# A fused linear-attention and FFN layer: the row sums of squares by one transpose instead of matmuls with ones

## The reference, cut to what matters

```python
xn = _layernorm(x)
x = x + attn(xn) + ffn(xn)
# attn, at its end; o, shift, final_gate: [B, T, 512]
o = gla_chunk_scan(q * SCALE, kn, v, rt_log)
o = o + shift * residual_weight
xg = o * silu(final_gate)
rms = rsqrt(mean(xg * xg, axis=-1) + 1e-5)
o = xg * rms * norm_weight
return o @ down_w.T
# ffn: three gated or plain layers of 1024, and w3 back to 256
```

## Time and profile before

| | us |
|---|---|
| median of 3 runs | 1967.26 |
| lowest, highest | 1966.08, 1968.8 |
| profiled execution, its own time | 1966.91 |
| its span, first to last instruction | 1965.0 |
| TensorE busy (matmuls) | 1947.1 |
| VectorE busy | 1581.9 |
| ScalarE busy | 1266.0 |
| GpSimd busy | 68.4 |

### The profile page before, as it was taken

How to read it: one execution, slowest core, us unless ns; L and a number is a source line. 1 busy time by engine, 2 the same in 40 slices (tenths; PEclk the granted TensorE clock), 3 DMA queues, 4 the chain that set the end, 5 groups by cost and what they waited for, 6 DMA issues and landing times.

```text
span 1965.0 us, 46591 instructions
## 1 busy us (share of the span) xinstructions
PE 1947.1 (99%) x17348; PEld 1932.8 (98%) x17348; DVE 1581.9 (81%) x4274; ACT 1266.0 (64%) x2527; POOL 68.4 (3%) x104
## 2 busy tenths in 40 slices
PE   7999999999999999999999999999999999999998
PEld 7999999999999999999999999999999999999998
DVE  7787878878788887887878788787888878878777
ACT  5665656666566666666656566666666666666564
POOL 0000000000000000000000000000000000000000
PEclk9999999999999999999999999999999999999999
DMA  8000000000000000000000000000000000000000
GB/s 305 7 12 12 12 7 6 12 12 12 12 1 12 12 12 12 12 1 12 12 12 12 7 6 12 12 12 12 1 12 12 12 12 12 2 12 12 12 7 8
DMA packets 23360, 34.22 MB, mean 17 GB/s; under 512 B 2945, under 2 KB 19713, under 8 KB 23186
## 3 DMA queue, kind: packets, MB, share of 16 engines
q1 hardware_dynamic: 23186, 31.46, 4.8%
HBM read 23.07 MB, written 8.39 MB: 16 GB/s over the span
## 4 chain that ended last, share of the span: by engine, by line
PE 95%; issue 2%; DVE 1%; ACT 1%; SPq 1%; DMA 0%; POOLq 0%; POOL 0%; DVEq 0%; ACTq 0%
PE fb L364 64%; PE ab L364 22%; PE ab L568 2%; PE ab L601 1%; PE ab L509 1%; PE ab L498 1%; PE ab L434 1%; PE fb L649 1%; PE ab L561 0%; SPq L272 0%; PE ab L580 0%; DVE hid0l L944 0%; PE ab L560 0%; DMA small<-stage_w 0%; ACT raw L805 0%
## 5 line engine op out<-in xcount | busy, mean ns | idle before, releaser
L364 PE MATMUL fb<-hid1h,wwhole 128*128 128x256 f32 x2048 | 475.0, 280 | 1.1 <-DVE hid1l L861 1.1
L364 PE MATMUL fb<-hid1l,wwhole 128*128 128x256 f32 x2048 | 468.5, 277 | 0.0
L364 PE MATMUL fb<-hid0l,wwhole 128*128 128x256 f32 x2048 | 465.9, 276 | 0.0
L364 PE MATMUL fb<-hid0h,wwhole 128*128 128x256 f32 x2048 | 465.8, 276 | 0.0
L364 PEld LDWEIGHTS fb<-hid1h,wwhole 128*128 128x128 f32 x2048 | 384.7, 188 | 3.8 <-ACT hid1h L720 0.8
L364 PEld LDWEIGHTS fb<-hid1l,wwhole 128*128 128x128 f32 x2048 | 384.9, 188 | 0.0
L364 PEld LDWEIGHTS fb<-hid0l,wwhole 128*128 128x128 f32 x2048 | 384.6, 188 | 0.0
L364 PEld LDWEIGHTS fb<-hid0h,wwhole 128*128 128x128 f32 x2048 | 384.5, 188 | 0.0
L805 ACT ACTIVATE raw<-fb,sh_s 128x256 f32<-128x256 f32 x512 | 212.7, 467 | 127.0 <-PE fb L364 124.8
L364 PE MATMUL fb<-xntl,wwhole 128*128 128x256 f32 x1024 | 237.5, 277 | 0.0
L364 PE MATMUL fb<-xnth,wwhole 128*128 128x256 f32 x1024 | 237.5, 277 | 0.0
(11 more groups left out here) (217 smaller groups left out, 4514.0 us busy)
## 6 DMA issues: line engine op xcount, KB each, us to landing
xin<-x SPq DMA_DIRECT2D x32, 256.0 KB, 2.7
out<-xin SPq DMA_DIRECT2D x32, 256.0 KB, 2.6
stage_more<-stage_w SPq DMA_DIRECT2D x6, 512.0 KB, 7.3
sgate<-stage_w SPq DMA_DIRECT2D x4, 512.0 KB, 5.5
shift<-stage_w SPq DMA_DIRECT2D x4, 512.0 KB, 5.6
v<-stage_w SPq DMA_DIRECT2D x4, 512.0 KB, 5.8
raw<-stage_w SPq DMA_DIRECT2D x3, 512.0 KB, 6.1
mixed<-stage_w SPq DMA_DIRECT2D x3, 512.0 KB, 8.5
```

Source lines behind the costliest of these rows:

```text
L364: mm = pe.matmul(o, a, b, start=start and i == 0, stop=stop and i == len(pairs) - 1)
```

## The change

The squares are written as two groups of 64 partitions. `sq` becomes [128, 8, 128]: partitions 0 to 63 hold chunk 0 and partitions 64 to 127 chunk 1, and the eight blocks are the four channel blocks of either half of the source's partitions. This takes four Squares of 64 partitions and 4 x 128 elements, for chunk c and source half r. VectorE then reduces eight blocks to `sqsum`, now [128, 128]: partition k of group c holds a partial sum of chunk c for each token. One fp32 transpose puts the tokens on the partitions and the 2 x 64 partial sums along them, in `fb[1]`, and a second VectorE reduction, out of PSUM, gives `total`, [128, 2]. `msq` is made from `total`, behind a wait for it. The bank `fb[1]` is read by the reduction and no longer by `msq`; TensorE still waits for `msq_d` before it writes there.

```diff
-        sq = work[:, 0:DB * N].rearrange("p (d t) -> p d t", d=DB)
+        sq = work[:, 0:NC * DB * CH].rearrange("p (d t) -> p d t", d=NC * DB)
         xn = work[:, DB * N:DB * N + NC * H].rearrange("p (c h) -> p c h", c=NC)
-        sqsum = work[:, DB * N + NC * H:]
+        sqsum = work[:, DB * N + NC * H:DB * N + NC * H + CH]
...
+        total = sb("total", [P, NC])
...
-        sq_d, xg_hi, ln_hi = sig("sq_d", 1), sig("xg_hi", 1), sig("ln_hi", 1, 1)
+        sq_d, xg_hi, ln_hi = sig("sq_d", NC * NC), sig("xg_hi", 1), sig("ln_hi", 1, 1)
...
-        sqsum_d = sig("sqsum_d", 1)
+        sqsum_d, total_d = sig("sqsum_d", 1), sig("total_d", 1)
...
                 pe.wait_ge(sqsum_d.sem, sqsum_d.at(me))
                 pe.wait_ge(gelu2_d.sem, gelu2_d.at(me, 4))
-                for c in range(NC):
-                    mm = pe.matmul(fb[1][:, c:c + 1], sqsum[:, c * CH:(c + 1) * CH], ones[:, 0:1], start=True, stop=True)
-                mm.then_inc(rs_mm.sem, 1)
+                pe.transpose(fb[1][:, 0:P], sqsum, ident_s[:]).then_inc(rs_mm.sem, 1)
...
-                act.activation(sq[:], sgate[:], ACT.Square).then_inc(sq_d.sem, 1)
+                for c in range(NC):
+                    for r in range(NC):
+                        act.activation(sq[rows(c), r * DB:(r + 1) * DB, :], sgate[rows(r), :, c * CH:(c + 1) * CH],
+                                       ACT.Square).then_inc(sq_d.sem, 1)
...
                 dve.wait_ge(rs_mm.sem, rs_mm.at(me))
-                dve.tensor_scalar(msq[:], fb[1][:, 0:NC], 1.0 / DI, EPS, ALU.mult, ALU.add).then_inc(msq_d.sem, 1)
+                dve.tensor_reduce(total[:], fb[1][:, 0:P].rearrange("p (c k) -> p c k", c=NC), mybir.AxisListType.X,
+                                  ALU.add).then_inc(total_d.sem, 1)
+                dve.wait_ge(total_d.sem, total_d.at(me))
+                dve.tensor_scalar(msq[:], total[:], 1.0 / DI, EPS, ALU.mult, ALU.add).then_inc(msq_d.sem, 1)
```

## The result

The changed kernel takes 1971.42 us (median of 14 runs, 1967.67 to 1974.03), the kernel before in the same session 1967.8 (14 runs, 1966.08 to 1968.8). The ratio is 1.0018, with a 95% interval of 1.001 to 1.0025. So the change made the kernel slower by a little under 4 us, where 9.5 us of gain were forecast. The profiled execution took 1969.75 us with a span of 1968.0, 3.0 more than before.

What follows compares the result with a forecast made beforehand. TensorE, busy 1947.1 of 1965.0 us, was taken as the bound: 31 halves by 0.325 gain 10.1 us, less 0.6 for the tail, 9.5 off 1966.91, so 1957.4; with 0.35 to the median, 1957.8 us, range 1955.8 to 1962.5.

Steps and rivals of the forecast that it cites:

- Slack 0.37: First halves: the reduction ends at 109.34, a load could start at 109.41, TensorE needs it at 109.78; no wait.
- slack 0.6: Second halves: squares start at 164.63, passes at 169.46, 4.83 us later instead of 4.59, so TensorE does not wait.
- all of the 0.325: TensorE, end of each half: four ones passes of 0.45 us become one transpose of 0.125, gaining 0.325 us.
- the sums come 1.47 later: ScalarE: four Squares in sequence take 2.52 us against one of 1.05, so the squares are ready 1.47 us later.
- I take 1.62: VectorE's long reduction to 128 sums of eight, priced per sum: 1.62 us instead of 2.02, bounds 1.62 to 2.15.
- Rival 1: VectorE's long reduction keeps its length or grows, 2.02 to 2.15 us, delaying TensorE in first halves; 1958.7 to 1960.9; chance 0.32.
- The switch to the next half's 16-column loads I price at nothing: TensorE, from the transpose to the next half's first loads: no added cost, as behind the ones passes.
- The tail: Last half, no TensorE work behind it: VectorE's path sets the end, msq at 1960.15 instead of 1959.60, 0.55 us later.
- the PSUM reduction: VectorE's new reduction over 128 PSUM elements ahead of msq: 0.30 us, plus 0.06 for the wait between the two.
- what was said to catch up: VectorE's convolution taps, delayed to 114.3, end at 115.98, before the z low's input at 116.18; lateness gone within one stage.
- the second: ScalarE's four squares take 0.9 us each, so TensorE waits for the sums; 1975.3 us at 1.0 us later; chance 0.05.
- The third: TensorE gains little: the transpose costs as much as four passes, or its next wait returns the gain; 1967.9 us; chance 0.10.

Runs made afterwards that it cites:

- late-sums run: The kernel before, ones passes kept, with its one Square cut into four of 64 partitions; 1975.74 us against 1968.2, ratio 1.0033.
- half-squares: The changed kernel with squares of only half the source's partitions, two Squares and a reduction over four blocks; 1961.54 us against 1968.43, ratio 0.9955.
- two-transpose: The kernel before, one Square and 256 sums, with two transposes and a PSUM reduction replacing the ones passes; 1971.7 us, ratio 1.0006; again 1964.53, ratio 0.9972.
- squares-ahead run: The changed kernel with squares and reduction moved ahead of the next input's high and low parts; 1968.44 us against 1968.2, ratio 1.0002.
- side-by-side: The changed kernel with a token's eight squares adjacent, so the reduction reads neighbours and ScalarE writes at a stride; 2034.37 us, ratio 1.0332.
- rounded-ones: The kernel before with sums and ones in the short rounded format, one pass per chunk instead of two, no transpose; 1965.62 us, ratio 0.9972.

## Why the prediction was wrong

**The step that failed: "Slack 0.37. In the second half ... slack 0.6. No wait, so all of the 0.325 stays."** The slack was measured to the load that uses the sums. Ahead of a turn of the loop, the deadline is earlier: the next half starts 0.93 us behind the release of the last wait in the loop's body, and what stands between, one transpose or four passes, runs within that time. Before, the sums were ready 2.19 us ahead of the next half, and the sums come 1.47 later, as I had worked out. With 0.325 less of TensorE's work in between, 2.19 - 1.47 - 0.325 = 0.40 us would have been left. The turn wants 0.93, so 0.53 us are lost; measured are 0.57 (60.03 against 59.71 - 0.25). The late-sums run shows it with nothing else changed, the half-squares and two-transpose runs show it gone with early sums, the squares-ahead run moves the sums and the next half moves along, and the loop's exit, which takes no turn, doesn't lose it. Why a turn takes this long no record shows. The Trainium skill (Runtime: NRT & Kernel Launch, Instruction fetch mechanics) says that a taken branch whose target is not among the instructions at hand waits for a fetch; a fixed time behind the last wait agrees with that, and no run here varied the length of the loop.

**"I take 1.62" for the reduction was mis-sized: 2.01.** The reading as a price per sum was wrong; the half-squares and side-by-side runs show a price per strided read. Rival 1 had the size right and the place too small: its 0.03 us in first halves came out as 0.08, and it saw nothing at the turns. With 1.62 the sums would have been 0.39 earlier, and 0.14 of the 0.53 would still be lost at each turn.

**"The switch to the next half's 16-column loads I price at nothing" was mis-sized by 0.08 us** in each half. Of 0.325 us some 0.24 stay: first halves went from 59.49 to 59.25, and the half-squares run's second halves from 59.71 to 59.47.

**The tail was mis-sized**: from the last square's start the prediction put msq 0.55 later. It starts at 1961.76, which is 0.96 later from there (0.4 of it the reduction) and 1.02 from the first load of the last half. The store of the output behind it landed 3.8 us after its issue instead of 3.0, which no run explains.

**What held.** Four squares of 0.629 us (0.635 taken), the sums' lateness in front of the reduction, the transpose's load of 0.14 and its own place in the queue, the PSUM reduction of 0.288 (0.30 taken). msq is never waited for, and what was said to catch up does so. VectorE ahead of and at the stage of the earlier trace rows:

```profile
112.30 0.29 DVE L1184 TENSOR_REDUCE total<-fb 128x2 f32<-128x128 f32 x1
112.62 0.17 DVE L1187 TENSOR_SCALAR msq<-total 128x2 f32<-128x2 f32 x1
113.66 0.88 DVE L1191 SCALAR_TENSOR_TENSOR xin<-ab,rms,xin 128x256 f32<-128x256 f32 x2 [0.87 <-POOL rms L350]
114.46 1.66 DVE L974 SCALAR_TENSOR_TENSOR shift<-xbuf,convw_s,shift 128x256 f32<-128x256 f32 x4
116.15 0.42 DVE L863 TENSOR_TENSOR zs<-ab,zs 16x256 fp32r<-16x256 f32 x1
```

The taps run together. Counted from the half's first load, z's low part starts at 6.44 us instead of 6.30 (116.15 - 109.71, 116.51 - 110.21), and TensorE doesn't wait for it.

**The sum, as it came out**, in the profiled spans: first halves at -0.24 each make -3.9; four stretches +3.3; a stall of 2.1 us near the end that only the kernel before has, -2.1; second halves +0.31 at 14 turns, with the last exit that does not turn, +4.1; tail +1.8; start -0.3. That is +2.9, against 3.0 between the spans. Held against the forecast instead (-0.325 in every half, +0.55 in the tail), the 14 second halves with a turn cost 0.636 x 14 = 8.9 us more, the exit 0.1, the first halves 0.08 x 16 = 1.3, the stretches 3.3 and the tail 1.25, less 2.1 and 0.3: 12.5, where the profiled execution is 12.4 above its forecast of 1957.4.

That stall was in nobody's sum. In the straight code of the last sequence, 34 us into its first half, ScalarE stands idle with no cause shown, and TensorE then waits for what it delivers, so that this half lasts 61.67 us instead of 59.49. Before:

```profile
1872.67 0.84 ACT L805 ACTIVATE raw<-fb,sh_s 128x256 f32<-128x256 f32 x2 [1.82 <-issue]
```

It is no accident of one execution: all five traces of kernels with the one Square have it (1.71 to 1.82 us of ScalarE), and none of the eight traces of kernels with two or four Squares. Why is open. So some 2 us of the comparison with before speak for the changed kernel, and for the half-squares and squares-ahead runs, for a reason that has nothing to do with the transpose; without them the loss would be larger.

**Of the rivals,** the second had the right form, TensorE losing to late sums, with the wrong cause (slow squares) and the wrong place. The third came nearest in size, with 1967.9, which is luck: the turns, the stretches, the tail and the stall happen to add up to little. Its break behind the transpose is what the rows show at a turn, but it doesn't belong to the transpose: the late-sums run has it behind the four passes. Where the two-transpose and the rounded-ones kernels beat both (0.9972 in the session where they were measured together), the first of them was level with before in another session, so a gain of some 3 us is likely for these and not settled. What makes TensorE fall from one distance to the other is open: the late load is necessary in all that was seen of h1, not sufficient, and it doesn't explain the stretches elsewhere.

## What to carry to other kernels

A wait that stands right ahead of a loop's turn has its deadline at the release, not at its instruction: measure the time from release to the first instruction of the next iteration, and keep late results (here those that come less than some 0.93 us ahead of the next iteration) away from that place. Before making a producer later to make a consumer shorter, look for the variant that shortens the consumer alone, as the single-pass ones did here. And count what a cheaper instruction does to its neighbour's start: a quarter of the gain went there.

## What the runs showed of the chip that was not expected

- The turn on TensorE: 0.92 to 0.94 us (medians; single turns 0.83 to 1.00) from the end of the reduction that releases the last wait to the next iteration's first load, in five kernels.
- Passes of 256 columns, of the same form and at a granted clock of 1.00, follow each other at 113.3 or at 117.8 ns for some 18 us of the h1 layer and 6 at the half's end, which makes 0.8 to 0.9 us in a half. Four and eight more such halves make 3.3 of 4.2 us and 7.4 of 7.5 us between two traces of one program; executions without a trace differ by up to 11 us, most likely for the same reason.
- An idle time of 1.7 to 1.8 us on ScalarE in the straight code behind the loop, at one place, in all five traces of kernels with one Square and in none of the eight others.
- A strided fp32 read costs VectorE 1.81 ns per element instead of 1.04 (stride 512 bytes), and writes at a stride of 32 bytes cost ScalarE 1.24 us instead of 0.63 for 64x512.
